# Second attention of a fused transformer block: weighted probabilities and value products in quarters of TensorE's array

## What is computed

```python
def _L1_xattn_ref(q, kv, x_seqlens, Wq, Wk, Wv, Wo, q_norm_w, k_norm_w):
    DIM, HEADS, HEAD_DIM = (128, 16, 64)
    qh = (q @ Wq).reshape(b, l, HEADS, HEAD_DIM).transpose(0, 2, 1, 3)
    kh = (kv @ Wk)...; vh = (kv @ Wv)...
    qh = rms_norm(qh, q_norm_w)
    kh = rms_norm(kh, k_norm_w)
    scores = jnp.einsum('bhld,bhsd->bhls', qh, kh) * (1.0 / np.sqrt(HEAD_DIM))
    scores = jnp.where(mask, scores, NEG_INF)
    attn = jax.nn.softmax(scores, axis=-1)
    o = jnp.einsum('bhls,bhsd->bhld', attn, vh)
    return o.reshape(b, l, HEADS * HEAD_DIM) @ Wo

x = x + jnp.tanh(g_xattn[1]) * _L1_xattn_ref(_layernorm(x), ctx_1024, _lenS2, ...)
```

## Time and profile before

| | us |
|---|---|
| median of 3 runs | 2466.07 |
| lowest and highest | 2465.31, 2469.52 |
| the profiled execution | 2468.33 |
| its span | 2466.5 |
| PE busy | 2129.7 (86%) |
| DVE busy | 1666.3 (68%) |
| ACT busy | 884.2 (36%) |
| POOL busy | 617.2 (25%) |

### The profile page before, as it was taken

The page is one execution under the profiler, slowest core; times in us unless marked ns, Lnnn a source line. Parts: engine busy times, 40 slices in busy tenths (PEclk is TensorE's granted clock), DMA queues, the critical chain, the costliest instruction groups (busy, mean ns, idle before and its releaser), DMA issues. The chain is left out here.

```text
span 2466.5 us, 39208 instructions
## 1 busy us (share of the span) xinstructions
PE 2129.7 (86%) x12508; PEld 1172.4 (48%) x12531; DVE 1666.3 (68%) x3418; ACT 884.2 (36%) x1559; POOL 617.2 (25%) x835
## 2 busy tenths in 40 slices
PE   4759989899899879999999899699979999859965
PEld 2634444444444446666666544245544444325531
DVE  4856776676777657777777589567756656536668
ACT  3622112201211146666666455123322222223335
POOL 4641100110111144555555332222100000021201
PEclk8569999999999889999999999799979999979976
DMA  3403212221320331111111000000000000010001
GB/s 100 145 1 70 53 23 64 52 53 33 65 56 17 76 107 36 33 33 34 34 33 32 22 1 1 3 12 12 11 5 0 0 0 0 0 27 13 12 3 34
DMA packets 116410, 80.37 MB, mean 33 GB/s; under 512 B 92777, under 2 KB 111081, under 8 KB 111812
## 3 DMA queue, kind: packets, MB, share of 16 engines
q1 hardware_dynamic: 116292, 78.91, 13.2%
HBM read 55.08 MB, written 2.82 MB: 23 GB/s over the span
## 5 line engine op out<-in xcount | busy, mean ns | idle before, releaser
L1021 PE MATMUL l0f_acc<-l0f_z,w_all 128*128 128x512 f32 x512 | 238.0, 628 | 22.8 <-DVE l0f_z L1245 22.8
L913 POOL TENSOR_TENSOR l0f_v<-l0f_val,l0f_top 64x256 f32<-64x256 f32 x128 | 78.2, 611 | 521.0 <-DVE l0f_val L1205 513.5
L967 PE MATMUL l0f_work<-w_all,l0f_xs 128*128 128x512 f32 x384 | 187.3, 611 | 9.3 <-DVE l0f_val L1200 8.0
L1021 PEld LDWEIGHTS l0f_acc<-l0f_z,w_all 128*128 128x128 f32 x512 | 102.2, 201 | 158.2 <-issue 131.2
L241 POOL TENSOR_SCALAR var_eps<-mean_var 128x4 f32<-128x4 f32 (+1 forms) x64 | 14.6, 227 | 571.0 <-DVE mean_var L225 569.2
L2785 DVE TENSOR_TENSOR l2f_work<-l2f_work,l2f_pu 128x512 f32<-128x512 f32 x104 | 71.4, 687 | 120.5 <-ACT l2f_work L2696 118.9
L2283 PE MATMUL a_score<-keys_by_head,a_qT 128*64 128x512 f32 x512 | 142.7, 639 | 9.4 <-DMA keys_by_head<-w_all 9.4
L1205 DVE COPY_PREDICATED l0f_val<-l0f_oh,l0f_work 128x512 f32<-128x512 int32 x160 | 116.9, 731 | 46.1 <-PE l0f_work L967 28.8
L2696 ACT ACTIVATE l2f_work<-l2f_pg 128x512 f32<-128x512 f32 x104 | 62.1, 597 | 207.0 <-PE l2f_pc L2636 174.6
L2641 PE MATMUL l2f_acc<-l2f_work,w_all 128*128 128x512 f32 x208 | 107.8, 600 | 12.1 <-DVE l2f_work L2789 10.9
L1705 DVE TENSOR_REDUCE l1x_ms_k<-l1x_sq_k 128x8 f32<-128x512 f32 x64 | 43.9, 685 | 102.8 <-ACT l1x_sq_k L1591 102.7
(11 more groups left out here) (372 smaller groups left out, 4893.7 us busy)
## 6 DMA issues: line engine op xcount, KB each, us to landing
l0f_first_mask<-onehots SPq DMA_DIRECT2D x32, 512.0 KB, 5.7
w_all<-onehots SPq DMA_DIRECT2D x32, 512.0 KB, 11.8
l1x_v<-l1x_vr SPq DMA_DIRECT2D x256, 64.0 KB, 2.1
w_all<-in_weights SPq DMA_DIRECT2D x1, 4640.0 KB, 17.4
l0x_m_b<-running_max SPq DMA_DIRECT2D x16, 256.0 KB, 4.6
keys_by_head<-w_all SPq DMA_DIRECT2D x256, 8.0 KB
keys_by_head<-ctxT_all SPq DMA_DIRECT2D x256, 8.0 KB
w_all<-in_weights SPq DMA_DIRECT2D x1, 2500.5 KB, 9.1
```

Source lines behind the costliest of these rows:

```text
L913: nc.gpsimd.tensor_tensor(v2[a * SEQ:(a + 1) * SEQ, t % 2, b, :, a, :], val[r, t % 2, :, :].rearrange("p (c a) k -> p c a k", a=2)[:, :, a ...
L967: nc.tensor.matmul(value_banks[e % 3][:, :], xs[:, t * P:(t + 1) * P], ve[:, e, :], start=True, stop=True).then_inc(ve_done, 1)
L1021: nc.tensor.matmul(acc[:, :], oe[:, n % E, n // E, :], z[:, n % Z, :], start=(n == 0), stop=(n == C * E - 1)).then_inc(acc_done, 1)
```

## The change

The division moves from the result to the probabilities. VectorE multiplies `prob` by 1/sum in place, right behind `totals` (`scale_probs`), and TensorE's `turn_probs` waits for that (`prob_ready`), not for `exp`. `values` is turned round: the values (64 keys x 64 features of one head) are stationary, and `probT` of that head and sequence (64 keys x 64 tokens) moves. Each product uses 64 rows and 64 columns of the array: head a of the pair uses the rows and the columns of half a. The result has features on the partitions, so `turn_out`, `og`, `scale_out` and the zeroed blocks of `v2` with their memset are gone, and `copy_oT` reads `po` itself. `values` of a unit now waits until `copy_oT` of the unit before has read `po` (`oT_ready`); `turn_k` no longer waits for `oT_ready`, and `exp` no longer for `sum_done`.

```diff
-        v2 = sb("v2", [P, 2, 2, C, 2, HD])
+        v2 = sb("v2", [P, 2, 2, C, HD])
...
-                sp.wait_ge(v2_zero, count(2))
...
-                            sp.dma_start(v2[a * SEQ:(a + 1) * SEQ, j % 2, b, :, a, :],
+                            sp.dma_start(v2[a * SEQ:(a + 1) * SEQ, j % 2, b, :, :],
...
-                nc.gpsimd.memset(v2[:, :, :, :, :, :], 0.0).then_inc(v2_zero, 1)
...
                 def turn_k(n):
                     pe.wait_ge(nm_k_done, count(n + 1))
                     after(pe, kT_ready, n)
-                    after(pe, oT_ready, n - 2)
...
                 def turn_probs(n):
-                    pe.wait_ge(exp_done, count(n + 1))
+                    pe.wait_ge(prob_ready, count(n + 1))
...
                     pe.wait_ge(pT_ready, count(n + 1))
                     pe.wait_ge(v_loaded[j % 2], 64 * (4 * g + j // 2 + 1))
-                    after(pe, og_ready, n)
+                    after(pe, oT_ready, n)
+                    pe.sem_inc(may_multiply, 1)
                     for c in range(C):
                         for b in range(2):
-                            q = slice(b * SEQ, (b + 1) * SEQ)
-                            ins = nc.tensor.matmul(po[q, c * P:(c + 1) * P], probT[:, c, q],
-                                                   v2[:, j % 2, b, c, :, :].rearrange("p a e -> p (a e)"),
-                                                   start=True, stop=True)
+                            for a in range(2):
+                                r = slice(a * SEQ, (a + 1) * SEQ)
+                                q = slice(b * SEQ, (b + 1) * SEQ)
+                                ins = nc.tensor.matmul(po[r, c * P + b * SEQ:c * P + (b + 1) * SEQ], v2[r, j % 2, b, c, :],
+                                                       probT[r, c, q], start=True, stop=True)
                     ins.then_inc(pv_done, 1)
-
-                def turn_out(n):
-                    pe.wait_ge(og_ready, count(n + 1))
-                    pe.wait_ge(kT_ready, count(at_most(n + 3, U * GROUPS)))
-                    after(pe, oT_ready, n)
-                    for c in range(C):
-                        ins = nc.tensor.transpose(turn1[:, c * P:(c + 1) * P],
-                                                  og[:, 2 * c:2 * c + 2, :].rearrange("p a e -> p (a e)"),
-                                                  core.const("ident"))
-                    ins.then_inc(o_turned, 1)
...
                 def exp(n):
                     act.wait_ge(sub_done, count(n + 1))
                     after(act, p_turned, n)
-                    after(act, sum_done, n)
...
                 def copy_oT(g, j):
                     n = U * g + j
-                    act.wait_ge(o_turned, count(n + 1))
+                    act.wait_ge(pv_done, count(n + 1))
...
-                                         turn1[:, :].rearrange("p (c q) -> p c q", c=C), ACT.Copy).then_inc(oT_ready, 1)
+                                         po[:, :].rearrange("p (c q) -> p c q", c=C), ACT.Copy).then_inc(oT_ready, 1)
...
-                def scale_out(n):
-                    dve.wait_ge(pv_done, count(n + 1))
+                def scale_probs(n):
                     dve.wait_ge(inv_done, count(n + 1))
-                    after(dve, o_turned, n)
-                    nc.vector.tensor_tensor(og[:, :, :], heads(po[:, :]), bcast(inv[:, :], 2, HD), ALU.mult)\
-                        .then_inc(og_ready, 1)
+                    nc.vector.tensor_tensor(prob[:, :, :], prob[:, :, :], bcast(inv[:, :], 2, SEQ), ALU.mult)\
+                        .then_inc(prob_ready, 1)
...
                     if live(h):
                         totals(U * h + i)
+                        scale_probs(U * h + i)
...
-                    h, i = lagging(g, j, 2)
-                    if live(h):
-                        scale_out(U * h + i)
```

More of the change, by code:

```diff
@@ L1311, in l1_xattn @@
         probT = sb("probT", [P, C, P])
-        og = sb("og", [P, HU, HD])
         oT = sb("oT", [P, 2, 2 * C, PAIR])
@@ L1329, in l1_xattn @@
         sum_done, inv_done, may_scale = sem("sum_done"), sem("inv_done"), sem("may_scale")
-        p_turned, pT_ready, pv_done, og_ready = sem("p_turned"), sem("pT_ready"), sem("pv_done"), sem("og_ready")
-        o_turned, oT_ready = sem("o_turned"), sem("oT_ready")
+        p_turned, pT_ready, pv_done, prob_ready = sem("p_turned"), sem("pT_ready"), sem("pv_done"), sem("prob_ready")
+        oT_ready, may_multiply = sem("oT_ready"), sem("may_multiply")
         y_done, yT_ready, y_turned, res_done = sem("y_done"), sem("yT_ready"), sem("y_turned"), sem("res_done")
@@ L1560, in slot @@
                         turn_probs(U * h + i)
-                    h, i = lagging(g, j, 3)
-                    if live(h):
-                        turn_out(U * h + i)
                     h, i = lagging(g, j, 1)
@@ L1733, in totals @@
                     dve.wait_ge(sum_done, count(n + 1))
-                    after(dve, og_ready, n)
+                    after(dve, prob_ready, n)
                     nc.vector.reciprocal(inv[:, :], tot[:, :]).then_inc(inv_done, 1)
-                def scale_out(n):
-                    dve.wait_ge(pv_done, count(n + 1))
+                def scale_probs(n):
                     dve.wait_ge(inv_done, count(n + 1))
-                    after(dve, o_turned, n)
-                    nc.vector.tensor_tensor(og[:, :, :], heads(po[:, :]), bcast(inv[:, :], 2, HD), ALU.mult)\
-                        .then_inc(og_ready, 1)
+                    nc.vector.tensor_tensor(prob[:, :, :], prob[:, :, :], bcast(inv[:, :], 2, SEQ), ALU.mult)\
+                        .then_inc(prob_ready, 1)
                 def add_to_x(pair):
```

## The result

| us | before | after |
|---|---|---|
| median (lowest to highest) of 4 runs each | 2466.41 (2465.31 to 2469.52) | 2508.69 (2505.43 to 2512.61) |
| profiled execution, its span | 2468.33, 2466.5 | 2512.61, 2510.8 |

The account below looks back on a forecast made before the run. TensorE's own work was taken to set the pace, with other engines close behind. New waits of 0.55 + 1.16 + 0 + 0 = 1.71 us per four slots, 16 times, add 27 us: 2493 us from 2466.07, range 2480 to 2510.

Parts of the forecast that it names:

- The mechanism: TensorE waits for the multiply ahead of `turn_probs`, and `values` for `copy_oT`: +0.55 us in kind 1, +1.16 in kind 2.
- `turn_out`'s time is not won in the long slots: Long slots: the 0.46 us of `turn_out` are not won, as `scores` needs `copy_kT` and `values` needs `copy_oT`; taken as 0.
- TensorE's own work sets the pace: Middle of the stage before the change: TensorE, busy 39.42 of 40 us, was taken as what sets the pace.
- The products, 1.04: `values` on TensorE: 32 passes of 64 columns take 1.04 us, 0.07 more than the 0.97 before.
- `turn_probs` 0.97 late in kind 1, 1.39 in kind 2: Short slots on TensorE: `turn_probs` waits for sum, reciprocal and multiply, and starts 0.97 us late in kind 1, 1.39 in kind 2.
- `values` 0.09 behind `copy_oT`: Hand-over from ScalarE to TensorE: `values` starts 0.09 us after `copy_oT` of the unit before ends.
- The change of shape at nothing, because TensorE stands idle there: Ahead of `values`: the array's change from 128 x 64 to 64 x 64 costs 0, covered by TensorE's idle time.
- The allowances: Ahead of `values`, upper bound only: 0.09 us each for shape change and semaphore instruction, 2.4 for four slots, +39 us, 2505.
- TensorE as the bound (2441): Faster rival: the waits don't bite, missing `turn_out` wins 0.39 us in each slot, 25 us, 2441; chance 0.07.
- both of its conditions: Scaled probabilities 0.97 us sooner in kind 1 and 1.39 in kind 2 than forecast, and `copy_oT` 0.4 sooner in all four.
- Quarters in turn (2551): Slower rival in `values`: the two array quarters take turns, products take 1.94 us, 0.90 more per slot, 2551; chance 0.08.

Follow-up runs that it names:

- the new order: Changed kernel, `copy_oT` and `exp` first on ScalarE, sum and multiply first on VectorE, `add_to_x` in kind 1, `turn_k` ahead of `project_v` in long slots: 2452.56 us.
- The best order: Changed kernel in the new order, with GpSimd's two staging copies also moved to the start of kind 3: 2445.11 us, ratio 0.9907.

## Why the prediction was right

The measured 2508.69 lies above my 2493, above the 2505 of my own upper bound, and inside 2480 to 2510 by 1.3 us only, thanks to the little that I had added on that side. The mechanism held, the size was short: 1.71 us for four slots against 2.35. Point by point:

- *`turn_out`'s time is not won in the long slots.* Right. They kept 8.78 and 8.95, held by the mask and `copy_oT`. With the new order 0.23 of it is, in each.
- *TensorE's own work sets the pace,* with which the prediction starts. Not quite: in the kernel before, each long slot became 0.41 us shorter when `turn_k`, and with it `copy_kT`, came earlier (with `exp` and the sum first, but `turn_k` in its old place, it was still 8.77). The prediction saw that `turn_out` waits for `copy_kT`, and did not price it.
- *The products, 1.04.* 1.08 from their start to the next `project_q`. Small, but it is paid in all four slots: +0.04 x 4. Passes of 18 and of 64 moving columns so take nearly the same, as I had it; that the weight loads set the time, and not the issue of the instructions, no run shows.
- *`turn_probs` 0.97 late in kind 1, 1.39 in kind 2.* 0.95, and in kind 2 it starts 5.55 into the slot against my 5.52. The chain through sum, reciprocal and multiply was right to 0.03, and taking the multiply out gave back 33 us. In every second slot of kind 1 the slow hand-over to `turn_probs` adds 0.16, which is 0.08 on average. In kind 2 it is 0.69 from `turn_probs` to `copy_pT` where I had 0.64, and 0.50 from there to `copy_oT` where I had 0.47.
- *`values` 0.09 behind `copy_oT`.* This is the term that was too small. It held in kinds 0 and 2 (0.11 and 0.10), but in kinds 1 and 3 the step is 0.25, 0.16 more in each: 0.32 of the 0.64 us that four slots took beyond my sum. I took the step from one row of one hand-over (`copy_kT` to `turn_out`, rows 7). That the added semaphore instruction fills the gap is not shown, as said above.
- *The change of shape at nothing, because TensorE stands idle there.* True in all four kinds, in kind 2 only just: `copy_oT` ends at 1141.12 there and `values` starts 0.10 behind it, while TensorE by itself would have been ready 1.03 behind `scores`, at 1141.17. The 0.10 for shape or increment is paid only where `copy_oT` is early.
- *The allowances.* I kept both for the upper bound, 0.09 each in every slot, which made 2.4 for four, 39 us and 2505. The slots grew by 2.35. That the two agree is chance: neither the shape nor the increment is seen to cost anything in kinds 0 and 2. What the sum lacked is made up of the slow hand-overs (0.32 and 0.08), the products (0.16) and small steps in kind 2.
- *The rivals.* TensorE as the bound (2441) failed on both of its conditions. The best order comes near that figure with 2445, but by luck: 13 us of it are the order's, and of the 0.39 a slot that this rival priced, 0.23 came in the long slots. Quarters in turn (2551): excluded in the changed kernel, and 2555 when brought about by hand. By the rule in the Trainium skill (TensorEngine Tiling (Array Packing), Gotcha 1: PSUM Pressure), that different row tiles cannot access the same PSUM bank at the same time, the changed kernel would have been at the second figure; the measured 1.08 for 32 passes against 1.79 speaks against it for quarters that write different partitions of the bank.

Outside the 63 slots 1.9 us are less ahead and 6.3 more behind them (1094.8 against 1088.5). 2.3 of the 6.3 are in the last steps of the stage, up to the last residual's addition. The rest is unchanged code, and over the profiled executions of all kernels here that part takes between 1057.4 and 1063.4 us. The first slots of the stage hold some more: the third of kind 2 takes 9.88 us, 1.4 more than later ones, with the cause open.

## What to carry to other kernels

An engine that is busy 99% of the time need not be all that bounds the kernel: here a new order alone won 13 us, and when work was taken from it, the next engine's copy, 0.2 us behind, became the bound. Moving an operation from the end of a chain to its middle costs its length only if what it stands ahead of is waited for, so look first at where in each engine's queue the chain runs, and reorder the queues before judging the change. Count each semaphore instruction that you add behind the wait that ends last. And take the length of a hand-over from several rows of the loop: here it had two values, 0.10 and 0.25, in fixed places.

## What the runs showed of the hardware

- Two 64 x 64 quarters of TensorE's array that differ in rows and columns and write different partitions of one PSUM tile computed at once when their products alternated in the queue, and not when all of one quarter stood first: 1.08 us against 1.79 for the same 32 passes of 64 columns, where passes one behind the other on the whole array come to 1.72 (an estimate from `project_v`, 0.86 for two passes of 512 columns).
- Each of two increments of a semaphore that were added in TensorE's own queue behind a wait took 0.15 us, not hidden by anything (2528.10 against 2508.69 us).
- From the start of products of 128 x 64 to that of products of 64 x 64, with one increment between them, TensorE took about 0.10 us more than without both (1.03 against 0.92).
- TensorE started 0.10 or 0.25 us behind the copy that it waited for (0.06 or 0.24 behind the multiply), always the same in the same slot of the loop; the cause is open.
